# Second attention of a two-block transformer: the turn of the normalised tokens by VectorE and a bounce through DRAM instead of by TensorE

## The reference

```
m, v = mean(x), var(x)                       # per token, over 256 channels
x_mod = (x - m) * rsqrt(v + 1e-6) * (1 + scale_msa) + shift_msa
k, q, v = split(x_mod @ w_qkv, 3)            # 16 heads of 16 channels
w = softmax(q / 16 @ k.T)                    # per head, 256 x 256
y = w @ v
x = x + gate_msa * (y @ w_proj + b_proj)
```

## Time and profile before

| | us |
|---|---|
| median of 3 runs | 1591.31 |
| lowest, highest | 1590.36, 1597.63 |
| the profiled execution, its own time | 1586.12 |
| its span, first to last instruction | 1584.3 |
| TensorE busy in the span | 1552.9 (98%) |
| VectorE, ScalarE, GpSimd busy | 1292.5, 874.4, 386.5 |
| mean granted TensorE clock | 0.992 of full speed |

### The profile page before, as it was taken

The page is one execution under the profiler, slowest core; times in us unless marked ns, Lnnn a source line. Parts: engine busy times, 40 slices in busy tenths (PEclk is TensorE's granted clock), DMA queues, the critical chain, the costliest instruction groups (busy, mean ns, idle before and its releaser), DMA issues.

```text
span 1584.3 us, 42381 instructions
## 1 busy us (share of the span) xinstructions
PE 1552.9 (98%) x14314; PEld 1394.6 (88%) x14314; DVE 1292.5 (82%) x2953; ACT 874.4 (55%) x1753; POOL 386.5 (24%) x525
## 2 busy tenths in 40 slices
PE   8999999999999999999999999999998999999999
PEld 7999998999999998777777777777775999999999
DVE  5798888687777777788888888888886788888886
ACT  3566664444444454667677766777765444444443
POOL 2333322010000012234344334344332300000000
PEclk9999999999999999999999999999998999999999
DMA  6700002211111111333333333233331232333332
GB/s 177 217 21 20 20 20 66 72 43 47 46 46 46 46 47 55 102 108 114 99 104 106 101 109 109 96 106 106 103 107 62 81 97 94 99 99 93 99 98 69
DMA packets 147505, 132.84 MB, mean 84 GB/s; under 512 B 23568, under 2 KB 130128, under 8 KB 147424
## 3 DMA queue, kind: packets, MB, share of 16 engines
q1 hardware_dynamic: 147264, 131.74, 26.4%
q0 software_dynamic: 160, 0.04, 0.0%
HBM read 54.75 MB, written 24.54 MB: 50 GB/s over the span
## 4 chain that ended last, share of the span: by engine, by line
PE 92%; DVE 4%; issue 2%; ACT 1%; DMA 1%; DVEq 0%; SPq 0%; POOL 0%; POOLq 0%; ACTq 0%
PE bank L209 64%; PE bank L1756 8%; PE bank L1738 7%; PE bank L1700 5%; PE bank L1766 2%; PE bank L393 2%; PE bank L1774 1%; PE bank L765 1%; PE bank L465 1%; PE bank L191 1%; PE bank L556 0%; DMA A_w_film<-in_L_cond_film_w 0%; DVE C_negmax L1712 0%; DVE m_xhat L1712 0%; DVE B_g_hi L1099 0%
## 5 line engine op out<-in xcount | busy, mean ns | idle before, releaser
L1847 ACT ACTIVATE C_probs<-bank 128x1024 f32<-128x1024 f32 x256 | 262.4, 1025 | 159.1 <-PE bank L1738 158.7
L1712 DVE TENSOR_REDUCE C_negmax<-bank 128x4 f32<-128x1024 f32 x248 | 303.3, 1223 | 48.1 <-PE bank L1700 44.4
L1091 ACT ACTIVATE B_g<-bank,B_bias 128x256 f32<-128x256 f32 x256 | 107.4, 471 | 207.4 <-PE bank L209 207.4
L1091 ACT ACTIVATE D_g<-bank,D_bias 128x256 f32<-128x256 f32 x256 | 107.3, 471 | 196.8 <-PE bank L209 196.7
L358 POOL TENSOR_TENSOR m_small<-m_small,consts 128x2 f32<-128x2 f32 x64 | 47.6, 744 | 601.9 <-DVE m_small L352 307.6
L209 PE MATMUL bank<-B_wt_w_hi,B_g_lo 128*128 128x256 f32 x512 | 144.7, 283 | 3.2 <-DVE B_g_lo L1101 3.1
L1738 PEld LDWEIGHTS bank<-C_qs,C_kx 64*128 64x128 f32 x1024 | 77.7, 186 | 78.8 <-ACT C_probs L1847 45.9
L209 PE MATMUL bank<-m_h_hi,B_wt_w_lo 128*128 128x256 f32 x512 | 143.6, 280 | 0.0
L209 PE MATMUL bank<-B_wt_w_hi,B_g_hi 128*128 128x256 f32 x512 | 143.3, 280 | 0.0
L209 PE MATMUL bank<-B_wt_w_lo,B_g_hi 128*128 128x256 f32 x512 | 143.3, 280 | 0.0
L209 PE MATMUL bank<-m_h_lo,B_wt_w_hi 128*128 128x256 f32 x512 | 143.3, 280 | 0.0
(11 more groups left out here) (267 smaller groups left out, 4842.1 us busy)
## 6 DMA issues: line engine op xcount, KB each, us to landing
C_qs<-C_q_hi SPq DMA_DIRECT2D x128, 128.0 KB
C_kx<-C_k_hi SPq DMA_DIRECT2D x128, 128.0 KB, 2.6
C_qs<-C_q_lo SPq DMA_DIRECT2D x64, 128.0 KB
C_kx<-C_k_lo SPq DMA_DIRECT2D x64, 128.0 KB, 2.1
C_gbc<-mod_rows SPq DMA_DIRECT2D x32, 256.0 KB, 3.4
D_gbc<-mod_rows SPq DMA_DIRECT2D x32, 256.0 KB, 3.4
turned<-N_blocks SPq DMA_DIRECT2D x31, 256.0 KB, 2.0
N_back<-turned SPq DMA_DIRECT2D x124, 64.0 KB, 2.0
```

What stands on the lines that cost most here:

```text
L1091: ins = eng.activation(o, p, func, bias=per_seq(bias1, 2 * u + d, b))
L1712: e_max.by(eng.tensor_reduce(m4[:, :, :, j], spair[:, :].rearrange("p (e q k) -> p e q k", e=2, q=TH), AX, ALU.max, negate=True))
L1847: e_exp.by(eng.activation(probs[t % NP][:, :], stpair[:, :], ACT.Exp, scale=scl))
```

## The change

For sequences 2 to 31 stage C leaves out T and does what stages B and D do: turn on VectorE (behind mt0 in the round), turn out and turn back on SP, and hi_h, lo_h from the tile that came back (`back` is a tile of the MLP's normaliser that stands idle; `blocks` is new). hi_h moves on ScalarE from due time 15.465 to 18.7, which is from in front of exp6 to in front of exp0 of the next round of its loop; lo_h0 moves on VectorE from in front of out0 to in front of lo_h1. In SP's round "turn out" (6) stands behind md0 and "turn back" (10.5) behind k1. The tokens of q, k and v stand in the turned order; softmax and the sums over k don't depend on it, and the order of the queries is restored in Y0 and Y1, which become two copies of half a tile each with a permuted read and write.

```diff
-            def evac_lo(self, eng, b):
+            def evac_lo(self, eng, b, parts=range(KT)):
...
-                for t in range(KT):
+                for t in parts:
...
-                n.e_lo.by(ins)
+                if KT - 1 in parts:
+                    n.e_lo.by(ins)
...
+                blocks, back = sb("blocks", [P, TH * D]), mlp_norm.lo[1][:, :].bitcast(F32)
...
-                T_PE = {"T": 8.873, "k": 15.427, "q": 23.777, "S0": 31.014, "S1": 33.045, "S2": 34.555, "v": 35.681,
+                T_PE = {"k": 15.427, "q": 23.777, "S0": 31.014, "S1": 33.045, "S2": 34.555, "v": 35.681,
...
-                T_ACT = {"hi_h": 15.465, "hi_k": 23.929, "hi_q": 26.206, "vout": 40.131, "exp0": 51.08, "exp1": 51.093,
+                T_ACT = {"hi_h": 18.7, "hi_k": 23.929, "hi_q": 26.206, "vout": 40.131, "exp0": 51.08, "exp1": 51.093,
...
-                T_DVE = {"stats": 0.622, "lo_h0": 8.331, "lo_h1": 9.442, "lo_k0": 18.476, "lo_k1": 18.622,
+                T_DVE = {"stats": 0.622, "turn": 6.25, "lo_h0": 9.43, "lo_h1": 9.442, "lo_k0": 18.476, "lo_k1": 18.622,
...
-                T_SP = {"z0": 13.302, "k0": 18.822, "q0": 23.053, "z1": 25.59, "k1": 25.869, "q1": 32.649, "md0": 36.928,
+                T_SP = {"turn out": 6, "turn back": 10.5, "z0": 13.302, "k0": 18.822, "q0": 23.053, "z1": 25.59, "k1": 25.869, "q1": 32.649, "md0": 36.928,
...
+                turn = Turn(norm, event, UNROLL, blocks, back)
...
-                NORMED = ("stats", "root", "xhat", "T", "hi_h", "lo_h0", "lo_h1")
+                NORMED = ("stats", "root", "xhat", "turn", "turn out", "turn back", "hi_h", "lo_h0", "lo_h1")
...
-                    tasks = {"T": lambda b: norm.transpose(eng, b),
-                             "q": lambda b: qk_cm(eng, b, "q"),
+                    tasks = {"q": lambda b: qk_cm(eng, b, "q"),
...
-                        e_ysb.by(eng.activation(ysb[w][:, :], ybank[:, :], ACT.Copy))
+                        if not turn.turns(b):
+                            e_ysb.by(eng.activation(ysb[w][:, :], ybank[:, :], ACT.Copy))
+                            return
+                        y4 = ysb[w][:, :].rearrange("p (g h a i) -> p h g a i", g=2, h=TH, a=QUADS)
+                        b4 = ybank[:, :].rearrange("p (g a h i) -> p h g a i", g=2, h=TH, a=QUADS)
+                        for h in range(TH):
+                            ins = eng.activation(y4[:, h], b4[:, h], ACT.Copy)
+                        e_ysb.by(ins)
...
-                    tasks = {"hi_h": lambda b: norm.evac_hi(eng, b),
+                    tasks = {"hi_h": lambda b: turn.evac_hi(eng, b),
...
+                    tasks = {"stats": lambda b: norm.stats(eng, b), "turn": lambda b: turn.turn(eng, b),
...
+                        tasks[f"lo_h{t}"] = lambda b, t=t: turn.evac_lo(eng, b, parts=(t,))
...
+                    tasks = {"turn out": lambda b: turn.send(eng, b), "turn back": lambda b: turn.fetch(eng, b),
```

More of the change, by code:

```diff
@@ L1547, in phase_l1_attention @@
                 NEXT_SP = {"D w2": 532, "D turn2": 550, "D gates": 555, "D gates1": 556}
-                BANK = {"T": 1, "q": 2, "k": 1, "v": 2, "Y1a": 2, "Y1b": 0, "Y2": 0, "PR": 0}
+                BANK = {"q": 2, "k": 1, "v": 2, "Y1a": 2, "Y1b": 0, "Y2": 0, "PR": 0}
                 pe_order = schedule(0, T_PE)
@@ L1561, in phase_l1_attention @@
                 head_bank = misc[1]
-                norm = Norm(attention_norm, event, False, scale1a, mbank("T"), (e_v, 1), centred=True)
+                norm = Norm(attention_norm, event, False, scale1a, head_bank, (e_v, 1), centred=True)
+                turn = Turn(norm, event, UNROLL, blocks, back)
                 freed = {"v": (e_vev, 1), "Y1a": (e_ytok, 1), "Y1b": (e_ytok, 2),
-                         "T": (norm.e_lo, 1), "Y2": (e_yf, 1), "q": (e_loq, 1), "k": (e_lok, 1), "PR": (e_tmp, 1)}
+                         "Y2": (e_yf, 1), "q": (e_loq, 1), "k": (e_lok, 1), "PR": (e_tmp, 1)}
                 def bank_free(eng, name, b):
@@ L1950, in gated @@
                             e_tmp.by(ins)
-                    tasks = {"stats": lambda b: norm.stats(eng, b),
+                    tasks = {"stats": lambda b: norm.stats(eng, b), "turn": lambda b: turn.turn(eng, b),
                              "ms0": lambda b: max_split(b, 0), "ms1": lambda b: max_split(b, 1),
@@ L1956, in vector @@
                     for t in range(KT):
-                        tasks[f"lo_h{t}"] = lambda b, t=t: norm.evac_lo(eng, b, parts=(t,))
+                        tasks[f"lo_h{t}"] = lambda b, t=t: turn.evac_lo(eng, b, parts=(t,))
                         tasks[f"lo_q{t}"] = lambda b, t=t: lo_bias(eng, b, "q", parts=(t,))
@@ L2068, in d_gates @@
                         heads["D"].load_gates(eng, seq)
-                    tasks = {"gates": load_gates, "D w2": d_w2, "D turn2": d_turn, "D gates": lambda b: d_gates(b, FIRST),
+                    tasks = {"turn out": lambda b: turn.send(eng, b), "turn back": lambda b: turn.fetch(eng, b),
+                             "gates": load_gates, "D w2": d_w2, "D turn2": d_turn, "D gates": lambda b: d_gates(b, FIRST),
                              "D gates1": lambda b: d_gates(b, SECOND)}
```

## The result

| | before | after |
|---|---|---|
| median of 5 runs, us | 1591.31 | 1845.60 |
| lowest, highest | 1584.13, 1598.35 | 1838.56, 1851.97 |
| the profiled execution, own time; span | 1586.12; 1584.3 | 1838.56; 1836.8 |

The changed kernel takes 1.163 times as long (95% interval 1.157 to 1.170): 254 us more, where 225 had been forecast (1816 us, range 1755 to 1880). Stages A, B and D take next to no part in the difference. The spans differ by 252.5 us. The first y_lo of the second attention (a step on GpSimd, one for each sequence) comes 16.5 us later, and from the first to the last of the 32 it takes 804.5 us instead of 567.1; together that is 254 us, and the rest of the span is 1.3 us shorter.

The account below looks back on a forecast made before the run. TensorE was taken to bound the kernel, busy for 98% of the span. Stalls of 6.0 us for 30 sequences (180 us) plus 45 us of clock loss made 225 us, added to the median: 1816 us, range 1755 to 1880.

Parts of the forecast that it names:

- The ring: Second attention: closed loop of waits from mt0 through SP, landing, hi_h, exp0, ST1 to next mt0; 24.0 us against 18.0.
- Paid in every sequence: Second attention: the 6.0 us stall recurs for each of 30 sequences, 180 us.
- The lower end of the range: Two sequences at either end not stalled and no clock loss: 28 x 5.8 = 162, 1753, rounded to 1755.
- The clock: TensorE behind each stall: the clock falls anew, 1.5 us a sequence, 45 us over 30.
- My bounds: Clock loss per stall on TensorE: 0 if the clock stays or slow work has slack, at most 3.1 us.
- The sum: Whole kernel: 180 us of stalls plus 45 us of clock, 225 us, giving 1816 us.
- signs: Second attention: a period of 25 to 26 us, and ScalarE idle before hi_h for 5 to 6 us.
- T is worth nothing here: TensorE: T's 0.58 us isn't on the ring; S5's wait for max4 behind turn fills its place.
- The edits at nothing: Split copies Y0, Y1, reads from SBUF and lo_h0's move cost nothing; added DMA at most 0.6 us a sequence.
- 1 (clock holds, 1771): Second attention: same stall, but the clock holds or its loss is hidden; 1591 + 180 = 1771 us; chance 0.14.
- 2 and 3 (hidden): Trip hidden: either TensorE's period shrinks, 1574 us, chance 0.07, or VectorE eats the gain, 1594 us, chance 0.05.
- 4 (half clock along the whole half ring): Clock at half along the whole 10.7 us of TensorE's and VectorE's part; 2032 us at most, some 1950; chance 0.05.

Follow-up runs that it names:

- early_fetch: Changed kernel with turn back at due time 7.0 instead of 10.5 on SP, right behind turn out, ahead of q0, z1, gates and k1: 1685.85 us.
- hi_later: Changed kernel with hi_h on ScalarE behind exp0 of sequence i-2 instead of in front of it: 1817.38 us.
- no_bounce: Changed kernel without turn out and turn back; hi_h and lo_h read the blocks that VectorE's turn left: 1594.64 us.
- round_early: Changed kernel with everything but normalising, turn and its DMAs one round later, hi_h and lo_h0 at their due times of before: 1604.98 us.
- hi_later_q0_first: Changed kernel with hi_h behind exp0 on ScalarE and turn back on SP at 7.5, behind q0, ahead of z1 and k1: 1662.94 us.
- busy_stall: Changed kernel with 48 matmuls of unread result on TensorE between AV3 and ST1, filling the stall: 1787.99 us.
- round_early_turn14: round_early with turn on VectorE moved from behind mt0 to in front of max1, its two SP tasks moving with it: 1591.46 us.
- re14_first4: round_early_turn14 with sequences 2 and 3 left to TensorE's T as before: 1583.94 us.

## Why the prediction was right

**The ring: right, link by link.** Turn back stood right behind k1 and did not wait for turn out. The rows give 936.56 - 928.38 = 8.18 us from mt0's end to its issue (7.92 worked out), data at 940.12 (938.10 for the last issue, by the chain, and 2.02) and so 11.74 us (11.25), and ST1 at 942.20, 13.82 us behind (13.35; before 7.34). The other half, TensorE's and VectorE's own work, is 928.38 - 915.29 = 13.09 us; 10.7 plus the clock had been 12.2. Together 26.91. That both orders matter is shown by early_fetch and hi_later; that little else does, by no_bounce and round_early.

**Paid in every sequence: right**, 30 waits. The lower end of the range had spared two sequences; none was. The 16.5 us at the start are the first two stalls.

**The clock: the term that was mis-sized.** I took 1.5 us a period from a single short fall; the ring's half grew by 13.09 - 10.68 = 2.41 us, and the run with the filled stall gives 1.9 (58 us by 30) to 2.2. Behind a stall of 6.4 us the clock stayed low for most of 7 us, not 3.5. My bounds, 0 and 3.1, held it. Where stalls were as short as those of the earlier trace rows (hi_later_q0_first, early_fetch), a fall did cost 1.5 us: 21.6 - 20.15 and 22.0 - 20.5. The Trainium skill (TensorE: Matmul & The Clock Gate, HAM oscillation) says of its kernel that the loss is paid in each tile; by busy_stall and the 0.82 of a whole period, the trace agrees for long stalls, while behind short ones it was paid in some periods only.

**The sum.** Measured are 252.5 us of span, 8.4 for each of the 30 stalls; forecast were 6.0 + 1.5. The ring is 0.5 us longer than worked out (SP's gaps, and the four issues of turn back at 0.49 instead of 0.43 us each) and the clock takes 0.9 more. So the period of 26.8 and hi_h's wait of 6.55 us lie above what was given as signs (25 to 26, and 5 to 6). Against that stand 0.5 us which the forecast counted too much: in the kernel before, the period isn't set by the ring's 7.34 + 10.68 = 18.02 us but is 18.20 in the mean, and the sequences at the ends seem to pay less (not looked at one by one). So errors of both signs are in the total, which is 28 us off the forecast.

**T is worth nothing here: right, but the reason given was only a small part.** The prediction let S5's wait for max4 fill T's place. TensorE of the changed kernel, in the stretch of the rows above:

```profile
929.85 0.50 PE L1741 MATMUL bank<-C_qs,C_kx 64*128 64x256 f32 x4 [0.33 <-ACT C_probs L1849]
930.19 0.46 PE L1703 MATMUL bank<-C_kx,C_qs 64*128 64x256 f32 x4
```

What waits is ST6, for exp5 on ScalarE: 0.33 us, and in no_bounce, round_early and round_early_turn14 about 0.3 in every period, while the kernel before has no such wait. S5 follows 0.34 us behind ST6, as it does in the kernel before, and 1.81 us behind mt0's end (forecast 1.95, before 1.89). A wait of S5 for max4 shows only in every second period of no_bounce and round_early, where S5 comes about 0.40 and 0.63 us behind ST6. In no_bounce the period is 18.13, with T gone and turn in front of max4; with turn elsewhere it is 17.98, and there S5 is always 0.34 us behind ST6. So turn's place took some of what could be had (0.15 us against no_bounce, 0.28 against round_early; why these differ wasn't tried), and of T's 0.58 us no run got back more than 0.22.

**The edits at nothing: right.** Split copies and reads from SBUF in no_bounce: nothing that can be told. Traffic: at a period of 18.26 the DMA share in round_early is 0.41 for 0.33, and the period differs from no_bounce's by 0.13 us: 4 us at most.

**The rivals.** 1 (clock holds, 1771) is the case that busy_stall builds: 1788, the 17 us more being the 0.5 us by which the ring was under-counted, 30 times. 2 and 3 (hidden) came true only in round_early and its variants, 1584 to 1605, after the ring had been cut; none gained the 17.4 us of rival 2. 4 (half clock along the whole half ring) falls by the same windows: clock 0.55 over the first 7 us, and from 949.6 on an S takes 0.42 us again instead of 0.63. The Trainium skill's advice for TensorE in such transposes (VectorE: DVE Perf Modes, Rules for kernel authors) stood against the change and was borne out for this placement; but the trade as such is no loss: with the trip hidden and turn elsewhere the two ways of transposing are equal within 0.4% (round_early: 0.7%).

## What to carry to other kernels

When a step is replaced by one with a long latency, don't compare work with work: put the new wait's place in every in-order queue beside the loop that the pipeline closes, and count from the ring's last link to its next. The latency of this trip was free at the distance of one more round (period 18.26 us for 18.20), and cost over 8 us a sequence without it. And when a queue is reordered to make one item earlier, price each item that it passes, by the time at which its reader wants it.

## What the runs showed that I had not expected

**Two paces of the same matmuls at the same granted clock.** The MLPs of both blocks run either at 852 or at 885 matmuls in 100 us, both at a granted clock of 1.00 with TensorE busy throughout. Of the twelve profiled executions four have the slow pace in the first MLP and the quick one in the second (the kernel before and the changed one among them, so the 252.5 us owe nothing to it), two the reverse, five the slow one in both, one the quick one in both. Windows in the first and the second MLP, of the kernel before, hi_later_q0_first and re14_first4 in turn:

```profile
350.00:450.00 100.00, 100.00 (x852) 100.00 (x851) 74.89 (x178) 40.82 (x97) 8.10 (x10) 1.00 0.14 45
1400.00:1500.00 100.00, 100.00 (x885) 100.00 (x884) 84.15 (x194) 42.97 (x103) 6.97 (x9) 1.00 0.31 97
```

```profile
350.00:450.00 100.00, 100.00 (x882) 99.93 (x881) 78.29 (x185) 42.06 (x100) 7.93 (x10) 1.00 0.15 48
1450.00:1550.00 100.00, 100.00 (x885) 100.00 (x884) 83.33 (x194) 42.72 (x101) 7.34 (x9) 1.00 0.31 99
```

```profile
350.00:450.00 100.00, 100.00 (x852) 100.00 (x850) 74.73 (x178) 40.54 (x96) 8.01 (x10) 1.00 0.15 47
1400.00:1500.00 100.00, 100.00 (x852) 100.00 (x851) 79.97 (x186) 41.52 (x99) 6.89 (x9) 1.00 0.28 92
```

From the last y_lo to the end the span has 346 to 349 us at the quick pace (before, after, no_bounce) and 360 to 361 at the other (round_early, round_early_turn14): 13 us, about 3.7% of such a stage. That would fit the steps in the times of the kernel before, which lie at 1575 to 1577, 1583 to 1592 and 1595 to 1603 us. What picks the pace wasn't tried. It limits what medians can tell: the profiled round_early had the slow pace in both MLPs, which may be part of the excess over its range, and so did the profiled re14_first4 (1598.02 us, 14 above its median); the 0.4% of re14_first4 may be in part such a difference too. Differences of periods inside the stage don't suffer from it.

**Short stalls and the clock.** Behind equal stalls of 1.7 us of TensorE the clock fell in some periods and held in others (4 of 20 in hi_later_q0_first), and a fall cost some 1.45 us; what decides stays open.
